# The inverse root of the first layer norm: GpSimd's power against ScalarE's root and VectorE's reciprocal

## The reference

```python
x = L0_attn_x                                   # 1 x 4096 x 512, float32
x = _layernorm(x + _L0_attn_ref(x, Wq, Wk, Wv, Wo), axis=-1)   # linear attention, then x @ Wo.T
x = _layernorm(x + _L0_ffn_ref(x, ...), axis=-1)               # Hadamard, gate/up, silu, Hadamard, down

def _layernorm(x, axis=-1, eps=1e-05):
    m = jnp.mean(x, axis=axis, keepdims=True)
    v = jnp.var(x, axis=axis, keepdims=True)
    return (x - m) / jnp.sqrt(v + eps)
```

## Time and profile before

| | |
|---|---|
| median of 3 runs | 2302.7 us (2302.54 to 2304.26) |
| profiled execution, its own time | 2305.09 us |
| its span, first to last instruction | 2303.3 us |
| second stage, about | 930 to 1322 us of the span |
| TensorE busy | 98% of the span |
| VectorE, ScalarE, GpSimd busy | 80%, 55%, 49% |
| instructions of the inverse root (L1326) | 32, together 34.7 us on GpSimd |

### The profile page before, as it was taken

The page is one execution under the profiler, slowest core; times in us unless marked ns, Lnnn a source line. Parts: engine busy times, 40 slices in busy tenths (PEclk is TensorE's granted clock), DMA queues, the critical chain, the costliest instruction groups (busy, mean ns, idle before and its releaser), DMA issues.

```text
span 2303.3 us, 32900 instructions
## 1 busy us (share of the span) xinstructions
PE 2255.0 (98%) x10209; PEld 1823.8 (79%) x10209; DVE 1833.8 (80%) x2484; ACT 1274.2 (55%) x2285; POOL 1118.6 (49%) x1002
## 2 busy tenths in 40 slices
PE   7999999999999999999999999999999999999998
PEld 5778787787878787788888778888888888888887
DVE  7877777778786868788888896787888788878877
ACT  6666666666676767233344555454545455554543
POOL 4667776767676767455544732321342133303321
PEclk9999999999999999999999999999999999999999
DMA  4110201111110215767767541323223322222323
GB/s 153 38 65 37 69 32 69 41 65 54 47 69 32 73 41 197 269 237 250 261 231 261 192 142 55 124 83 110 83 96 96 115 87 92 92 83 83 100 65 101
DMA packets 132701, 252.75 MB, mean 110 GB/s; under 512 B 44576, under 2 KB 45344, under 8 KB 122880
## 3 DMA queue, kind: packets, MB, share of 16 engines
q1 hardware_dynamic: 132608, 251.60, 32.5%
HBM read 188.11 MB, written 63.44 MB: 109 GB/s over the span
## 4 chain that ended last, share of the span: by engine, by line
PE 72%; issue 11%; POOL 9%; DVE 5%; ACT 2%; DMA 1%; POOLq 0%; ACTq 0%; DVEq 0%; SPq 0%
PE pj L550 17%; PE pj L631 10%; PE pnum L631 6%; PE pj L645 5%; PE psc L631 5%; PE pj L560 4%; PE pst L631 4%; PE psc L645 4%; PE pnum L645 3%; PE psc L581 3%; PE pnum L599 3%; PE pnum L602 3%; PE pst L645 2%; POOL fa L1343 1%; POOL fb L1344 1%
## 5 line engine op out<-in xcount | busy, mean ns | idle before, releaser
L1373 POOL TENSOR_TENSOR wcs<-wcr 128x256 f32<-128x256 f32 x64 | 67.9, 1060 | 513.9 <-DVE wcl L1112 504.8
L1406 POOL TENSOR_TENSOR tb<-tb,sinb 128x512 f32<-128x512 f32 x160 | 224.2, 1402 | 91.4 <-ACT tb L930 90.6
L550 PE MATMUL pj<-xah,wqh 128*128 128x512 f32 x512 | 204.2, 399 | 4.1 <-DVE Kf L1248 1.8
L1409 POOL TENSOR_TENSOR Ql<-tb,Qh 128x512 fp32r<-128x512 f32 x128 | 170.2, 1332 | 69.7 <-ACT Qh L939 69.6
L478 PE MATMUL pj<-woh,oh 128*128 128x512 f32 x512 | 202.6, 396 | 0.0
L550 PE MATMUL pj<-xal,wqh 128*128 128x512 f32 x512 | 200.7, 392 | 0.0
L550 PE MATMUL pj<-xah,wql 128*128 128x512 f32 x512 | 200.5, 392 | 0.0
L478 PE MATMUL pj<-wol,oh 128*128 128x512 f32 x512 | 200.2, 391 | 0.0
L478 PE MATMUL pj<-woh,ol 128*128 128x512 f32 x512 | 200.1, 391 | 0.0
L1236 DVE TENSOR_TENSOR pj<-pj,cosb 128x512 f32<-128x512 f32 x160 | 111.2, 695 | 69.5 <-ACT tb L930 69.0
L929 ACT ACTIVATE tb<-pj 64x512 f32<-64x512 f32 x160 | 95.4, 596 | 112.9 <-PE pj L550 108.8
(11 more groups left out here) (258 smaller groups left out, 7090.6 us busy)
## 6 DMA issues: line engine op xcount, KB each, us to landing
num_scratch<-no SPq DMA_DIRECT2D x128, 256.0 KB, 2.4
nt<-num_scratch SPq DMA_DIRECT2D x32, 1024.0 KB, 5.5
rb<-rden_scratch SPq DMA_DIRECT2D x32, 1024.0 KB, 6.6
wdr<-wd_scratch SPq DMA_DIRECT2D x128, 256.0 KB, 3.3
wcr<-in_wg SPq DMA_DIRECT2D x64, 256.0 KB, 2.8
wcr<-in_wu SPq DMA_DIRECT2D x64, 256.0 KB, 3.1
xst<-in_xT SPq DMA_DIRECT2D x34, 256.0 KB, 3.7
xr<-in_x SPq DMA_DIRECT2D x32, 256.0 KB, 5.6
```

The lines of the kernel that those rows point to most:

```text
L550: last = nc.tensor.matmul(bank[:, :], w[:, b, :], x[:, b, :], start=(k == 0), stop=(k == 11))
L1406: nc.gpsimd.tensor_tensor(tb[c][:, :], tb[c][:, :], sinb[:, :], ALU.mult).then_inc(sin_done, 1)
L1409: nc.gpsimd.tensor_tensor(Ql[g % 2][:, c, :], (tb[c] if c else Kf)[:, :], f32(Qh[g % 2][:, c, :]), ALU.subtract).then_inc(lo_done, 1)
```

## The change

In the second stage, for chunks 0 to 30, the power on GpSimd and the addition of epsilon on VectorE go. ScalarE makes the root of variance plus epsilon (`deviation`), with epsilon as a bias operand, behind `upper` and ahead of `columns`. VectorE makes the reciprocal of it directly ahead of the norm. Chunk 31 keeps the old way: VectorE adds epsilon (`variance`) and GpSimd makes the power. The second layer norm, in the third stage, is not changed.

```diff
+            def deviation(n):                                   # ScalarE
+                act.wait_ge(ln_step, n * 2 + 2)
+                if not isinstance(n, int) or n:
+                    act.wait_ge(rstd_done, n)
+                nc.scalar.activation(dev[:, :], mv[:, 1:2], ACT.Sqrt, bias=eps[:, 0:1]).then_inc(dev_done, 1)
...
                 if at + 1 < NC:
                     upper(1 - s, n + 1, at + 1)
+                if at == 1:
+                    act.wait_ge(eps_set, 1)
+                if at >= 1:
+                    deviation(n - 1)
...
+            def variance(n):                                    # VectorE, chunk 31 alone
+                dve.wait_ge(ln_step, n * 2 + 2)
+                nc.vector.tensor_scalar_add(ve[:, :], mv[:, 1:2], EPS).then_inc(ve_done, 1)
...
-                dve.wait_ge(ln_step, n * 3 + 1)
+                dve.wait_ge(ln_step, n * 2 + 1)
                 nc.vector.sem_inc(passed, 1)
                 nc.vector.bn_aggr(mv[:, :], stats[:, :]).then_inc(ln_step, 1)
-                dve.wait_ge(ln_step, n * 3 + 2)
-                nc.vector.tensor_scalar_add(ve[:, :], mv[:, 1:2], EPS).then_inc(ln_step, 1)
 
             def norm(s, n):
+                if not isinstance(n, int) or n < NC - 1:
+                    dve.wait_ge(dev_done, n + 1)
+                    nc.vector.reciprocal(rstd[:, :], dev[:, :]).then_inc(rstd_done, 1)
                 dve.wait_ge(rstd_done, n + 1)
...
             def step(m, j, at):                                 # GpSimd
                 n = m * NCH + j
-
-                if at >= 2:
-                    inverse_root(n - 1)
-                if at == 0:
-                    inverse_root(0)
                 if j == 0:
                     scaled(m)
```

More of the change, by code:

```diff
@@ L246, in phases @@
         stats, mv, ve, rstd = little("stats", 6), little("mv", 2), little("ve", 1), little("rstd", 1)
+        dev, eps = little("dev", 1), little("eps", 1)
         sg, su2 = little("sg", FB), little("su2", FB)
@@ L293, in phases @@
         r_done = sem("r_done")
+        dev_done, ve_done, eps_set = sem("dev_done"), sem("ve_done"), sem("eps_set")
         ln_step, rstd_done, x1_ready = sem("ln_step"), sem("rstd_done"), sem("x1_ready")
@@ L1164, in gate_up @@
                     sums(1, NC - 1, NC // 2 - 1, NC - 1)
+                    variance(NC - 1)
                     columns_lo2(0, 2)
@@ L1324, in inverse_root @@
             def inverse_root(n):
-                pool.wait_ge(ln_step, n * 3 + 3)
+                pool.wait_ge(ve_done, 1)
                 nc.gpsimd.tensor_tensor(rstd[:, :], ve[:, :], neghalf[:, :], ALU.pow).then_inc(rstd_done, 1)
@@ L1425, in _ @@
             nc.gpsimd.memset(neghalf[:], -0.5).then_inc(zeroed, 1)
+            nc.gpsimd.memset(eps[:], EPS).then_inc(eps_set, 1)
             for s, tile in ((j_done, NR), (v_done, NCH), (t_done, KV), (dn_done, KV), (shifted, NR), (cos_done, NR),
```

## The result

The changed kernel is slower: 2307.56 us median of 21 runs (2305.61 to 2309.09), against 2304.24 us of 21 runs of the kernel before on the same chips (2301.29 to 2308.13). The ratio is 1.0015, 95% interval 1.001 to 1.0021, that is 2.3 to 4.8 us. The forecast was 2.7 us faster. The loss is small, 0.15%, but the interval lies clear of 1. The span of the profiled execution is 2306.5 us and was 2303.3, so 3.2 us more.

The account below looks back on a forecast made before the run. TensorE was taken as the bound, so only its empty moments could be won. Step 2 -3.4, steady tiles +2.9 and the third stage's start -2.2 made -2.7 us: 2300.0 from 2302.7, range 2294.5 to 2305.5.

Parts of the forecast that it names:

- the price of `lower` beside the folding: Step 0 of tiles 1 to 7: `lower` takes 3.44 us, transposes 0.32 us late a tile, 2.3 us lost.
- Step 2: Second stage, tile 0: folding starts earlier, transposes 0.9 us late, 1.8 us and 1.6 of slow clock regained, gain 3.4.
- Step 3: Step 3 of a tile: the reciprocal delays the norm by 0.28 us, times 6 is 1.7 us lost.
- Steps 1 and 2: Steady tiles: norm over a microsecond earlier, the lost 0.13 and 0.04 us come back, 1.1 us in all.
- The start of the third stage: Waits for split columns shrink: gain 1.67 + 0.5 + 0.54 = 2.7 us, 2.2 with the table load.
- the first wait: Start of the third stage: TensorE's wait of 1.67 us for split columns goes.
- the second wait: Start of the third stage: TensorE's wait of 3.04 us for split columns stays with 2.5, gain 0.54.
- the table load: ScalarE's added load for `Tanh`, where that engine is nearly full: 0.5 us lost, bounds 0 and 1.28.
- Rival C: Folding beside `lower` in step 0 costs 1.1 us a tile, reciprocal 0.67 in step 3: 2307.7 us, chance 0.1.
- Rival D: ScalarE loads tables in every chunk, two loads each, 7 us slower: 2307 us, chance 0.05.

Follow-up runs that it names:

- The two holds: Changed kernel with GpSimd's folding of tiles 1 to 7 held until the statistics, or until the norm, of chunk 4m-1: 2303.31 and 2299.35 us.
- The run with the moved power: Kernel before the change, with GpSimd's power of chunk 1 two instructions earlier, no longer behind tile 0's whole folding: 2303.61 us, ratio 0.9996.
- the changed kernel with `Exp`: Changed kernel with Exp in place of Sqrt for ScalarE's root, so the two added table loads go: 2308.01 us, ratio 1.0019.
- the run with the first hold: Changed kernel with GpSimd's folding of tiles 1 to 7 held until the statistics of chunk 4m-1: 2303.31 us, ratio 0.9995.

## Why the prediction was wrong

The view that TensorE is the bound and only its empty moments count held throughout. By the steps of the prediction:

- **The step that failed: the price of `lower` beside the folding.** The prediction took 3.44 us from the earlier trace rows as the price beside GpSimd and came to 0.32 us a tile. That row groups two halves, of which one was slowed. With both slowed it is 4.52 us, 1.1 us more. The norm behind it took 1.31 us and not the 1.5 of the forecast, so 0.32 + 1.08 - 0.2 = 1.2, and the transposes of step 0 do come 1.22 us late. Seven tiles make 7.4 us, not 2.3. The mechanism was right, its size was wrong by 5.1 us, and that turns -2.7 into +2.4. The two holds show the cause: with one half slowed 0.17 us are late, with none nothing is. A price for "beside GpSimd" was the wrong thing to look for: it goes by what GpSimd has under way when each half starts.
- **Why the power had protected `lower` was not seen.** In the kernel before the power runs beside the `lower` of the earlier trace rows, which starts at 1177.63 and keeps its 2.36 us. A power of 128 x 1 numbers did not slow VectorE there; the folding does. The power had been a placeholder that kept the folding away.

```profile
1177.77 1.50 POOL L1326 TENSOR_TENSOR rstd<-ve,neghalf 128x1 f32<-128x1 f32 x1 [13.91 <-DVE ve L1003]
```

- **Step 2.** Forecast: 0.9 us stay lost, 1.8 come back, and so does the slow clock, 3.4 in all. Measured: 1.22 stay, the clock does not fall, 3.1 in all. The run with the moved power shows that the place in GpSimd's list did it.
- **Step 3.** Forecast 0.28 us a tile for the reciprocal, measured 0.2 (0.42 for 0.23). The reciprocal itself takes 0.15 us, its wait 0.04, as taken.
- **Steps 1 and 2** lose nothing any more, as forecast.
- **The start of the third stage.** Forecast 2.2 us, regained 2.5, in part by luck. Norm 30 takes 0.55 us, as forecast, 0.5 us come back ahead of the transposes of chunk 30, as forecast, and 1.5 at the first wait, for 1.67. But the second wait gave 0.06 us and not 0.54 (2.98 us are left), the 0.5 us of the table load can't be told from nothing, and 0.5 us came back in step 30, for which the forecast had no term.
- **The end.** 1.4 us in the last 20 us of the profiled execution were in no step. ScalarE's wait of 2.56 us there is ended by a late DMA of `wdr`. Waits for that DMA, from 1.1 to 2.6 us in all, are found in every profile. The kernel before has 1.1; the run with only the moved power, which touches nothing there, has 2.6; the changed kernel with `Exp` has 1.2 and loses nothing at the end. So I do not count them to the change; no run tested it on its own.

As measured, -3.1 + 7.3 - 2.5 + 1.4 makes 3.1 of the 3.2 us by which the spans differ. Rival C, given 0.1, had the right sign and the right place, step 0. Its 2307.7 us are luck: it stood 5.0 above a kernel before of 2302.7, the measured time stands 3.3 above one of 2304.24, and the 0.67 us for the reciprocal that it also needs were 0.2. Rival D is out: there are three loads.

## What to carry to other kernels

Taking an instruction off an engine also takes away what it held back. Write down what stands behind it, when that will now start, and what the other engine does at that moment. And when a row groups several instructions, take them apart before their sum is used as a price, and look at what the other engine had under way when each of them started. Put the short instruction that the bound engine waits for ahead of the long one that it does not wait for yet; that made a change that lost 3 us into one that gains 9, though with the power on GpSimd the same order gave nothing.

## What the runs showed of the hardware

- VectorE's subtraction of two SBUF operands (128 x 1024) took 1.23 us alone and up to 2.32 beside GpSimd's folding, while the residual sum with one operand in PSUM kept its 0.68 us. The Trainium skill (GPSIMD Engine Reference, Key points) names two SBUF inputs as a case in which the two engines contend; the trace agrees. The norm, with one wide operand in SBUF, was slowed as well, from 0.55 to 1.31 us.
- Who is first counts. A half of `lower` that was under way 0.41 us ahead of GpSimd's instruction kept its 1.23 us, and GpSimd's two took 4.19 us instead of the 2.54 they took in the changed kernel, where they were ahead of `lower`. The other way round, each of the 26 halves that came second there ended 1.08 to 1.09 us after the end of GpSimd's instruction.
- TensorE's clock: after the wait of 2.55 us in step 2 of the kernel before, the granted clock fell from 1.00 to 0.50 (from the level of 2.4 to that of 1.2 GHz) between 962.6 and 966.0; after the 1.06 us of the changed kernel at the same place it did not fall, nor after 1.73 us there in the run with the first hold (1.00 from 960.5 to 964.0).
